# Four C products per chunk move from VectorE and GpSimd to ScalarE, by way of TensorE, in a fused adaLN + Mamba + FFN kernel

## The reference, cut to what matters

```python
dt = softplus(einsum('blr,er->ble', dt, dt_proj_w) + dt_proj_b)
A = -jnp.exp(A_log)
dA = jnp.exp(dt[..., None] * A)
dBu = (dt * h)[..., None] * Bp[:, :, None, :]
def step(s, xs):
    dA_t, dBu_t = xs
    s = s * dA_t + dBu_t
    return (s, s)
_, states = jax.lax.scan(step, s0, (dA.transpose(1, 0, 2, 3), dBu.transpose(1, 0, 2, 3)))
y = jnp.einsum('lben,bln->ble', states, Cp)
y = y + h * D
y = y * silu(gate)
return jnp.einsum('ble,he->blh', y, out_proj_w)
```

## Time and profile before

| | |
|---|---|
| median of 3 runs | 1928.72 us (1928.45 to 1929.2) |
| profiled execution, its own time | 1929.0 us |
| its span | 1927.3 us |
| VectorE busy | 1801.3 us, 93% |
| GpSimd busy | 1794.0 us, 93% |
| TensorE busy (matmul) | 1720.6 us, 89% |
| ScalarE busy | 1546.2 us, 80% |

### The profile page before, as it was taken

One profiled execution on the slowest core, in us unless ns is written; L12 is line 12 of the kernel. 1 busy time (PEld: TensorE's weight loads), 2 busy tenths in 40 slices (PEclk: granted clock), 3 DMA queues, 4 the chain that ended last, 5 costly groups with the idle time before them and its releaser, 6 DMA issues. The chain is left out here.

```text
span 1927.3 us, 29502 instructions
## 1 busy us (share of the span) xinstructions
PE 1720.6 (89%) x9176; PEld 1311.1 (68%) x9176; DVE 1801.3 (93%) x2260; ACT 1546.2 (80%) x4529; POOL 1794.0 (93%) x756
## 2 busy tenths in 40 slices
PE   7995998989899998998989899998989989899798
PEld 4664767667576766767677676766768676676664
DVE  3897999999999999999999999999999999999995
ACT  3776789798888979888787988879788897988773
POOL 1899999999999999999999999999999999999993
PEclk9897999999999999999999999999999999999899
DMA  5756514032140412304042340503213041321310
GB/s 179 258 115 157 145 51 163 24 128 82 55 143 20 152 50 100 110 23 164 23 153 66 116 148 23 165 23 137 72 72 127 34 152 35 104 78 44 111 28 33
DMA packets 72077, 186.17 MB, mean 97 GB/s; under 512 B 6896, under 2 KB 8560, under 8 KB 63984
## 3 DMA queue, kind: packets, MB, share of 16 engines
q1 hardware_dynamic: 68224, 176.94, 27.1%
q0 software_dynamic: 3696, 7.34, 2.4%
HBM read 172.20 MB, written 12.06 MB: 96 GB/s over the span
## 5 line engine op out<-in xcount | busy, mean ns | idle before, releaser
L604 POOL TENSOR_TENSOR ub<-u,b_all 128x2048 f32<-128x2048 f32 x255 | 1166.8, 4576 | 40.7 <-DMA b_all<-bc_scratch 40.7
L756 ACT ACTIVATE decay<-dt,decay_rate 128x256 f32<-128x256 f32 x2048 | 883.7, 465 | 20.4 <-DVE state_p L1548 1.1
L1548 DVE TENSOR_TENSOR_SCAN decay<-decay,ub 128x512 f32<-128x512 f32 x617 | 729.1, 1212 | 21.7 <-ACT decay L756 16.1
L620 POOL TENSOR_TENSOR sc_p<-state_p,c_all 128x1024 f32<-128x1024 f32 (+1 forms) x256 | 499.8, 1952 | 53.1 <-PE y_bank L1088 31.6
L1548 DVE TENSOR_TENSOR_SCAN state_p<-decay,ub 128x512 f32<-128x512 f32 x407 | 480.1, 1207 | 34.5 <-ACT decay L756 32.1
L1088 PE MATMUL y_bank<-ident,sc_d 128*128 128x128 f32 x2468 | 364.6, 279 | 103.6 <-DVE sc_d L1563 103.5
L1088 PEld LDWEIGHTS y_bank<-ident,sc_d 128*128 128x128 f32 x2468 | 289.0, 143 | 180.8 <-DVE sc_d L1563 127.4
L1563 DVE TENSOR_TENSOR sc_d<-decay,c_all 128x512 f32<-128x512 f32 x617 | 395.5, 675 | 7.4 <-PE y_bank L1088 1.7
L742 ACT ACTIVATE carry<-decay 128x2 f32<-128x2 f32 x617 | 99.8, 162 | 220.4 <-DVE sc_d L1563 219.0
L1170 PE MATMUL bank_a<-hT,win_h 128*128 128x256 f32 x992 | 236.3, 384 | 15.3 <-DVE hc L1612 7.8
L1088 PEld LDWEIGHTS y_bank<-ident,sc_p 128*128 128x128 f32 x1628 | 195.6, 145 | 65.5 <-issue 33.2
(11 more groups left out here) (137 smaller groups left out, 1813.3 us busy)
## 6 DMA issues: line engine op xcount, KB each, us to landing
win_h<-win_m SPq DMA_DIRECT2D x128, 256.0 KB, 2.6
win_z<-win_m SPq DMA_DIRECT2D x128, 256.0 KB, 2.7
b_all<-bc_scratch SPq DMA_DIRECT2D x31, 1024.0 KB, 4.7
c_all<-bc_scratch SPq DMA_DIRECT2D x31, 1024.0 KB, 5.1
xa<-x SPq DMA_DIRECT2D x16, 512.0 KB, 5.1
xc<-x SPq DMA_DIRECT2D x16, 512.0 KB, 3.8
out<-xc SPq DMA_DIRECT2D x15, 512.0 KB, 3.7
ffn<-factors POOLq DMA_DIRECT2D x7, 1024.0 KB, 10.1
```

What stands on the lines that cost most here:

```text
L604: pool.tensor_tensor(ub[:, slot, :, :, :], u[:, (PAIRS * c + q) % U_PAIRS, :, :].unsqueeze(1).to_broadcast([P, QUAD, 2, ROWS]), b_all[:, n ...
L620: pool.tensor_tensor(sc_p[:, slot:slot + k, :, :], state_p[:, slot:slot + k, :, :], c_all[:, n:n + k, :].unsqueeze(2).to_broadcast([P, k, ...
L756: last = act.activation(bk[:, j * ROWS:(j + 1) * ROWS], dt[:, pair % DT_PAIRS, j, :], ACT.Exp, scale=decay_rate[:, e, n:n + 1])
L1548: dve.tensor_tensor_scan(dst, bk[:, :], ub[:, quad % UB_RING, i, :, :].rearrange("p j r -> p (j r)"), 0.0, ALU.mult, ALU.add).then_inc(sca ...
```

## The change

In chunks 1 to 15, one unit in each pair (state n = 4, that is units 4, 20, 36 and 52, the first of quads 1, 5, 9 and 13) becomes an "ACT unit". Its scan writes to `state_a` in SBUF. TensorE turns the state (4 transposes) into the unit's decay bank, which is spent by then. There rows are on partitions, so C is one value per partition, and ScalarE multiplies it by the column `c_col` with two activations of 128x256 that write back to `state_a`. TensorE then adds it to `y_bank` with two 128x256 matmuls by the identity. The decay bank is free only after ScalarE's two activations. Once a chunk TensorE turns `bc_s` and ScalarE copies the C columns to `c_col`.

The pool table changes too, from 26 pool units a chunk to 24 in chunks 2 to 15, and the ring of `sc_d` goes from 4 to 3. VectorE makes 36 C products a chunk there, where it made 38; in chunk 1 it makes 4 fewer.

```diff
-D_RING = 4
+D_RING = 3
...
+A_RING = 1
+A_AT_UNIT = 0
+A_QUADS = (1, 5, 9, 13)
...
-EVERY_POOL = (2, 2, 1, 1, 2, 2, 1, 2, 2, 2, 2, 1, 2, 2, 1, 1)
+EVERY_POOL = (2,1,1,1,2,2,1,2,2,1,1,2,2,2,1,1)
...
 def freed_at(unit):
+    if on_act(unit):
+        return (unit | 1) + 0.7
     if not on_dve(unit):
         return unit
     return (unit | 1) + (0.6 if unit % 2 else 0.5)
...
+            def scale_turned(unit):
+                i, n, par = scaled_after(unit), unit % N, unit // UNITS % 2
+                act.wait_ge(state_turned, i)
+                act.wait_ge(carried, carries_after(unit))
+                act.wait_ge(c_col_made, unit // UNITS)
+                for t in range(LB):
+                    cols = slice(2 * t * P, 2 * (t + 1) * P)
+                    last = act.activation(state_a[:, (i - 1) % A_RING, cols], decay[bank_of[unit]][:, cols], ACT.Identity,
+                                          scale=c_col[:, par, t, n:n + 1])
+                last.then_inc(scaled_a, 1)
+
+            def copy_c_column(c):
+                act.wait_ge(c_turned, c)
+                wait(act, scaled_a, scaled_after(UNITS * (c - 1) - 1))
+                act.activation(c_col[:, c % 2, :, :], bank_a[1][:, 0:LB * 2 * N].rearrange("p (t n) -> p t n", t=LB)[:, :, N:],
+                               ACT.Copy).then_inc(c_col_made, 1)
...
             def decays(unit):
...
                     keep_carry(before)
                     if on_dve(before):
                         act.wait_ge(carried, carries_after(before))
+                    if on_act(before):
+                        scale_turned(before)
+                        act.wait_ge(scaled_a, scaled_after(before))
...
+                    if la is not None and s == 30:
+                        copy_c_column(c + 1)
                     if la is not None and s == 31:
                         tanh_gate(c, 0)
...
+            def turn_on_act(unit):
+                if on_act(unit):
+                    i, bk = scaled_after(unit), decay[bank_of[unit]]
+                    pe.wait_ge(scanned, unit + 1)
+                    for j in range(2):
+                        for t in range(LB):
+                            at = (2 * t + j) * P
+                            last = pe.matmul(bk[:, at:at + P], state_a[:, (i - 1) % A_RING, j * ROWS + t * P:j * ROWS + (t + 1) * P], ident[:, :],
+                                             start=(j == 0 and t == 0), stop=True, is_transpose=True, skip_group_check=True)
+                    last.then_inc(state_turned, 1)
+
+            def sum_on_act(unit):
+                if on_act(unit):
+                    i = scaled_after(unit)
+                    pe.wait_ge(scaled_a, i)
+                    for t in range(LB):
+                        cols = slice(2 * t * P, 2 * (t + 1) * P)
+                        last = pe.matmul(y_bank[:, cols], ident[:, :], state_a[:, (i - 1) % A_RING, cols],
+                                         start=False, stop=False, skip_group_check=True)
+                    last.then_inc(summed_a, 1)
...
                 if step % 2 or not first:
                     if step:
                         turn_on_dve(2 * step - 1)
+                    turn_on_act(2 * step)
+                    turn_on_act(2 * step + 1)
+                    if step:
+                        sum_on_act(2 * step - 2)
+                        sum_on_act(2 * step - 1)
                     turn_on_dve(2 * step)
...
+                    if la is not None and s == 30:
+                        turn_c_column(c + 1)
                     if c + 2 < CHUNKS and s == 31:
                         turn_x(c + 2, 0)
                         turn_x(c + 2, 1)
```

More of the change, by code:

```diff
@@ L107, in on_pool, with on_act @@
     return range(POOLED[quad]) if closes_pair(quad) else range(QUAD - POOLED[quad], QUAD)
+def on_act(unit):
+    quad, i = quad_of(unit)
+    return quad >= QUADS and i == A_AT_UNIT and quad % QUADS in A_QUADS
 def on_dve(unit):
     quad, i = quad_of(unit)
-    return i not in on_pool(quad)
+    return i not in on_pool(quad) and not on_act(unit)
 def ends_pool(unit):
@@ L134 @@
 DVE_COUNT = count(on_dve(u) for u in ALL_UNITS)
+ACT_COUNT = count(on_act(u) for u in ALL_UNITS)
 FREED = sorted(ALL_UNITS, key=freed_at)
-CARRIED_COUNT = dict(zip(FREED, count(on_dve(u) or ends_pool(u) for u in FREED)))
+CARRIED_COUNT = dict(zip(FREED, count(on_dve(u) or on_act(u) or ends_pool(u) for u in FREED)))
 def seam_count(c):
@@ L151, in products_after, with scaled_after @@
     return DVE_COUNT[unit]
+def scaled_after(unit):
+    return ACT_COUNT[unit] if unit >= 0 else 0
 def carries_after(unit):
@@ L257, in build @@
         sc_d = sb("sc_d", [P, D_RING, 2, ROWS])
+        state_a = sb("state_a", [P, A_RING, 2 * ROWS])
+        c_col = sb("c_col", [P, 2, LB, N])
         skipped = sb("skipped", [P, 2, 2, ROWS])
@@ L290, in build @@
         skip_turned, y_copied = sem("skip_turned"), sem("y_copied")
+        state_turned, scaled_a, summed_a = sem("state_turned"), sem("scaled_a"), sem("summed_a")
+        c_turned, c_col_made = sem("c_turned"), sem("c_col_made")
         ub_seamed, seam_decay, seam_made, marked = sem("ub_seamed"), sem("seam_decay"), sem("seam_made"), sem("marked")
@@ L735, in keep_carry @@
                     dst = carry[:, n, 2 * q:2 * q + 2]
+                elif on_act(unit):
+                    act.wait_ge(scanned, unit + 1)
+                    src = state_a[:, (scaled_after(unit) - 1) % A_RING, :].rearrange("p (j r) -> p j r", j=2)[:, :, ROWS - 1]
+                    dst = carry[:, n, 2 * q:2 * q + 2]
                 else:
@@ L847, in copy_y @@
                 act.wait_ge(turned_d, products_after(N * (pair + 1) - 1))
+                wait(act, summed_a, scaled_after(N * (pair + 1) - 1))
                 if pair == 0:
@@ L1097, in turn_on_dve, with turn_c_column @@
                     turn_state(sc_d[:, (i - 1) % D_RING, :, :], unit % N == N - 1).then_inc(turned_d, 1)
+            def turn_on_act(unit):
[17 more added lines that the diff above has]
+                    last.then_inc(summed_a, 1)
+            def turn_c_column(c):
+                pe.wait_ge(dt_made, PAIRS * (c + 1))
+                for t in range(LB):
+                    last = pe.transpose(bank_a[1][:, 2 * t * N:2 * (t + 1) * N], bc_s[:, t * P:(t + 1) * P], ident[0:2 * N, 0:2 * N])
+                last.then_inc(c_turned, 1)
             def turn_on_pool(quad):
@@ L1131, in turn_x @@
                 wait(pe, dt_made, PAIRS * c)
+                if j and c >= 2:
+                    pe.wait_ge(c_col_made, c - 1)
                 for i in range(2):
@@ L1295, in project_gate_last @@
                     pe.wait_ge(dt_made, PAIRS * CHUNKS)
+                    pe.wait_ge(c_col_made, FINAL)
                 elif j == 0:
@@ L1539, in scan @@
                     dst = bk[:, :]
+                elif on_act(unit):
+                    wait(dve, summed_a, scaled_after(unit) - A_RING)
+                    dst = state_a[:, (scaled_after(unit) - 1) % A_RING, :]
                 else:
```

## The result

| | before | after |
|---|---|---|
| median of 3 runs, us | 1928.72 | 2055.82 (2052.67 to 2055.99) |
| ratio, 95% interval | | 1.0654 (1.064 to 1.0669) |
| span of the profiled execution, us | 1927.3 | 2050.9 |

What follows compares the result with a forecast made beforehand. VectorE was taken as the bound, stalled in the steady part only by ScalarE. Terms of 2.0 + 0.55 + 0 + 1.9 = 4.45 us a chunk, thirteen times, plus chunks 0, 1 and 15, gave +64: 1993 us, range 1950 to 2022.

Steps and rivals of the forecast that it cites:

- the column: C column copy on ScalarE before the decay of unit 62 waits for TensorE: +1.9 us a chunk, chunks 0 to 14.
- signs of being right: Chunk period 118 or 119 us, stalls at unit 8 of each pair and unit 62, ScalarE waiting over 1 us at the copy.
- sign of being wrong: Period under 114, scaling pairs near 0.7, column turned before normalization ends, or VectorE stalled by `sc_d`'s ring or TensorE.
- What bounds the kernel: VectorE is the bound, GpSimd hard behind; only ScalarE stalls VectorE in the steady part, despite 17 us idle a chunk.
- The bank loop: Scalings delay the decay of unit 8 in each pair: its scan about 0.5 us later, four places, +2.0 a chunk.
- unit 59: Fourth pair, ScalarE without idle time: VectorE gets its whole lateness, 1.05 in place of 0.5, +0.55 us a chunk.
- What costs nothing: TensorE's added matmuls, 0.24 us each, 1.9 a chunk, are covered by 9.9 idle; `sc_d`'s ring of 3 is free.
- The third pair: Scan of unit 51 could come 1.1 us later as unit 45's decay waits for scan 43; 0 counted in the sum.
- (a): Rival: the chain before the scan of 56 is hidden and 20 us are kept, 1909 us; 1 in 10.
- (b): Rival: the column does not stall because TensorE is ahead there, +36, 1965 us; 15 in 100.
- (c): Rival: third pair's lateness kept whole, TensorE's clock low at half the columns, 2018 us, or 2029 at all; 17 in 100.
- (d): Rival: no change, the saved and the added meet within 0.2%; 2 in 100.

Runs made afterwards that it cites:

- e12: Kernel before with 24 pool units a chunk, quads 10 and 11 left at 2 and 1, same pool slots in all chunks: 1946.64 us, ratio 1.0096.
- e14: Changed kernel with late column copy, same slots in all chunks from 2 on, and quads 10 and 11 back at 2 and 1: 1978.26 us, ratio 1.026.
- e5: Changed kernel with the column copy behind the decay of unit 62 and every chunk from 2 on starting at slot 2: 1997.86 us, ratio 1.0356.
- e1: Changed kernel with the column copy moved behind the decay of unit 62: 2015.73 us, ratio 1.0448.
- e2: Changed kernel with every chunk from 2 on starting at slot 2 of the pool ring: 2045.39 us, ratio 1.0601.
- e6: e5 with one of the two scalings of each ACT unit left out: 1981.16 us, ratio 1.0271.
- e8: Changed kernel with late column copy, old pool table, and the ACT unit's bank given to the decay of unit 9 of the pair: 1974.27 us, ratio 1.0236.
- e7: e5 with TensorE's two adding matmuls of each ACT unit done twice: 2015.57 us, ratio 1.0454.
- e10: e5 with only one of TensorE's two adding matmuls of each ACT unit: 1983.41 us, ratio 1.0284.
- e4: Changed kernel without ACT units and with the old pool table; column turning and copy and the ring of 3 stay: 1956.3 us, ratio 1.0137.
- e11: Kernel before with only unit 20 as ACT unit, old pool table, late column copy and ring of 3: 1943.01 us, ratio 1.0073.

## Why the prediction was right in direction and off in size

The runs cut the 127.1 us into parts, each the difference of two kernels' times over before:

| part | us | from |
|---|---|---|
| two more products on VectorE by the table | 17.3 | e12 |
| four ACT units, the late column and the ring of 3 | 32.7 | e14 less e12 |
| quads 10 and 11 swapped | 18.6 | e5 less e14 |
| slots of the ring | 17.2 | e1 less e5 |
| column copy ahead of the decay of 62 | 41.3 | change less e1 |

The forecast's terms without the column were 64 - 28.5 = 35.5 us, against 17.3 + 32.7 = 50.0; the column was 15 x 1.9 = 28.5 against 41.3; the other two rows had no amount in it. The order in which the parts are removed matters (e2 gave 11.7 for the slots where the table has 17.2). The signs of being right came (stalls at unit 8 of each pair and at unit 62, ScalarE waiting for TensorE at the copy), but the period is 122 to 126 us in most chunks and not 118 or 119. One sign of being wrong came too, VectorE stalled by TensorE: 0.70 at a residual add of e5, 0.39 at the same place of the changed kernel.

**What bounds the kernel** held in part. ScalarE stalls VectorE through three banks: one scaling less gave 16.7 us (e6), and another unit for the bank moved the stall (e8). But I had called ScalarE the only engine that stalls VectorE, and the changed kernel has two more, GpSimd (23.8 us before scans to `state_p`) and, at a few places, TensorE (e7, e10).

**The bank loop** held. Against before, the start of the scans at unit 8 of the four pairs in chunk 12 moved by 0.6, 0.4, 0.7 and 0.7, where 0.5 each was forecast, and unit 59 by 0.49 more for 0.55. The scalings took 0.84 a pair, the lower bound of that term, not 1.0. That the chain came out so near is partly luck, since one other number was off the other way: a product moved up saves 0.38, not 0.64. The scan of unit 53 in the timelines of the kernel before and of the changed one:

```profile
1543.18 1.21 DVE L1548 TENSOR_TENSOR_SCAN decay<-decay,ub 128x512 f32<-128x512 f32 x1
...
1643.93 1.21 DVE L1640 TENSOR_TENSOR_SCAN decay<-decay,ub 128x512 f32<-128x512 f32 x1
```

Before, the first of two products starts 1.12 after that scan (1544.30 in the earlier trace rows). After, the product of 53 stands directly behind its own scan and starts 1.31 after it (1645.24), so 0.2 goes there. The rest is my 0.64, which is half of a pair's 1.27; from one product's start to the next is 1.27 - 0.68 = 0.59, and e12 shows 0.60 and 0.58. I take it that the product waits for the end of its scan (1645.14), which no run isolates. The Trainium skill's figures ("Perfetto Trace Analysis", "Optimizing Scalar/DVE Operations"), from which I had estimated 0.72 for a scaling pair, came nearer than my 1.0 but are under the measured 0.84. The estimate was two steps of 0.36. The measured pair is a step of 0.84 - 0.47 = 0.37 and then a whole record of 0.47 (the 471 ns of the group above), so the step agrees, and what the estimate lacked is that the second one's record is longer than its step.

**"What costs nothing" failed at TensorE.** I priced a matmul at 1.89 / 8 = 0.24 from a row with x8, but eight records there are four matmuls of the code, so one is 0.47 and a unit's two are 0.94, 3.8 us a chunk. And I set them against the 9.9 us of idle time in a chunk, the very sum over places that I had refused for ScalarE. At units 12 and 34 to 36 there is less room than 0.94: half of the adds gives back 14.5 us (e10). The terms without the column were short by as much (50.0 less 35.5 is 14.5), but the two need not be the same thing: the half was measured with the swap in place, and e14 with fewer adds was not run. In e14, chunk 12 is 3.72 longer than before. Of this, 2.35 stands at the four places (2.0 forecast), 0.52 at unit 59 (0.55 forecast) and 0.85 at units 12, 28 and 36, where the forecast had nothing.

**The third pair** had 0 in the sum and 1.1 as an upper bound, because GpSimd's share in quad 10 moved the decay of 45 behind the scan of 43. Between units 40 and 51 the scans of chunk 12 fell back by 1.0, some 14 us in 14 chunks, and taking the swap out was worth 18.6 (e14). The bound was right and the choice wrong: "a run of 16 us without a gap" was the reason to take it, and I used it as the reason to leave it out.

**The column** was mis-sized. Its 1.74 at full clock (e4) is my 1.9. I had the case of 3.6 from the earlier trace rows and took the other; measured, 3.42 in nine chunks of fifteen. The trace of the kernel before could have told me more: its projection at this place ran at the low clock in seven of the fifteen chunks, and I had looked at two. The ACT units make TensorE wait longer for the product of 58, 2.47 us in chunk 12 against 1.98 in the earlier trace rows. That the added wait brings the low clock is not shown: after 2.48 us the clock was at 1.00 in chunks 5, 8, 11 and 13, and with the same wait the projection was slowed in nine chunks of the changed kernel, thirteen of e2 and fourteen of e5. What decides it stays open.

**The slots** failed altogether: the prediction has no word on `slot_table`. It treated the table only as products moved between engines, but the table also sets which slots neighbours share. The earlier trace rows had the sign of it: 20.2 us of GpSimd's idle time before its products was released by TensorE's turning. In the kernel before this was off VectorE's path; with the new table it no longer was.

**The rivals.** (a) needed more than 1.1 us of room before the scan of 56; the scan waited 0.83 instead. That reading of the Trainium skill's "Perfetto Trace Analysis" (section "Identifying the Most-Contended Engine") would have been 1909. e8, which leaves all four products off VectorE, is the purest form of it, and is 45.0 us slower than before. (b) fell: the column stalled in every chunk. (c) was the nearest, and both of its mechanisms came, but even its 2029 is 27 too low: the slots and TensorE's adds are not in it. (d) fell. Chunk 0 took 1.8 more for 1.9, chunk 1 3.3 for 3.2, chunk 15 1.6 for 1. Chunk 1 is luck: its stall before unit 62 was 3.43 and not 1.9.

**Slips in the sums.** (b) takes away 14 columns where there are 15, and 14 x 1.9 from 64 leaves 37, not 36; with 15 it is 35.5. The range's lower end with a chain of 1.3 a chunk is 1965 - 13 x 0.7 = 1956, not 1950. Neither bears on the result.

No run beats the kernel before. The cheapest with ACT units in it is e11, with one, 13.7 slower. Placing the scalings elsewhere than at the four units, or a fourth decay bank, was not tried.

## What to carry to other kernels

Where a resource with few places (three banks, four slots) ties engines into a loop, the room at the tightest turn of the loop decides, for every engine in it, and idle time of a whole chunk is no cover for any of them. A table that moves work also re-deals the slots: work out the new deal over two periods, since a plan that repeated itself can begin to alternate, and neighbours then share a slot that did not before. Of a cost with two measured values, count in the whole trace how often each stands before taking one. And price a matmul from its count in the program, not from the count of records.

## What the runs showed of the hardware

- A projection of eight records of 128x256 took 3.50 us with TensorE's clock at 0.50 for most of it, in place of 1.89 at 1.00, and the stall that hung on it was 3.42 in place of 1.74. Both cases followed a wait of 2.47 or 2.48 us (chunks 12 and 11 of the changed kernel).
- A float32 matmul of 128x256 is two records of the trace, 0.47 us together (eight records and 1.89 us for four matmuls in e7; 240 records for 120 matmuls in the changed kernel). A 128x128 transpose is one record (x4 for the four of a unit, in the earlier trace rows).
- A VectorE product directly behind the scan that it reads started 1.31 us after that scan's start, where one behind the scan of another unit started 1.12 after it (units 53 and 52, changed kernel and kernel before).
- ScalarE's activation of 128x256 from PSUM to SBUF with a scale per partition has a record of 471 ns, and two in a row take 0.84, so the second starts 0.37 after the first.
